# 8-wide heads: three bank pairs in a ring for scores and turned scores, four row strips of scores at once, and the turned maximum in the projections' bank

## The reference

```python
q = (query @ Wq.T + bq).reshape(b, s, 16, 8).transpose(0, 2, 1, 3)   # k and v likewise, from the context
scores = einsum('bhqd,bhkd->bhqk', q, k) / sqrt(8)
scores = where(mask, scores, very_low)       # layer 0: |query - key| <= 64; layer 2: a mask that is an input
out = einsum('bhqk,bhkd->bhqd', softmax(scores), v)
x = x + out.transpose(0, 2, 1, 3).reshape(b, s, 128) @ Wo.T + bo
```

## Time and profile before

| | us |
|---|---|
| median of 3 runs | 2033.67 |
| lowest and highest of them | 2032.84, 2035.79 |
| span of the profiled execution | 2027.5 |
| PE, DVE, ACT, POOL busy in it | 1766.7, 1092.1, 891.5, 652.9 |
| weight loads (PEld) busy | 1258.1 |

### The profile page before, as it was taken

One profiled execution on the slowest core, in us unless ns is written; L12 is line 12 of the kernel. 1 busy time (PEld: TensorE's weight loads), 2 busy tenths in 40 slices (PEclk: granted clock), 3 DMA queues, 4 the chain that ended last, 5 costly groups with the idle time before them and its releaser, 6 DMA issues.

```text
span 2027.5 us, 48497 instructions
## 1 busy us (share of the span) xinstructions
PE 1766.7 (87%) x18886; PEld 1258.1 (62%) x18886; DVE 1092.1 (54%) x3147; ACT 891.5 (44%) x2432; POOL 652.9 (32%) x656
## 2 busy tenths in 40 slices
PE   6999985587869999998999971999699999999978
PEld 3565564576648778873565551999456666666753
DVE  4666657567532222214566763656465656665548
ACT  2333320476334444432333320666265555556525
POOL 3233201467311111103214426455133233333405
PEclk8999996788679999997999995999799999999969
DMA  5000000000000000007210001222200000000001
GB/s 174 7 13 8 2 2 9 28 16 1 1 6 1 1 2 2 1 1 293 104 76 18 18 18 45 61 57 58 90 17 17 17 17 17 6 1 1 1 1 42
DMA packets 48828, 63.55 MB, mean 31 GB/s; under 512 B 8106, under 2 KB 37701, under 8 KB 48349
## 3 DMA queue, kind: packets, MB, share of 16 engines
q1 hardware_dynamic: 44253, 51.98, 7.8%
q0 software_dynamic: 4352, 8.47, 1.3%
HBM read 32.29 MB, written 28.65 MB: 30 GB/s over the span
## 4 chain that ended last, share of the span: by engine, by line
PE 57%; DVE 9%; issue 7%; POOL 4%; POOLq 3%; DVEq 2%; ACT 1%; DMA 1%; SPq 1%; PEldq 0%; PEld 0%; ACTq 0%
PE single L1835 5%; PE quad L1823 5%; PE pair L570 3%; PE single L621 3%; PE single L2156 3%; PE quad L2139 2%; PE quad L2145 2%; PE pair L1796 2%; PE quad L598 2%; PE pair L2519 2%; POOL tokens_by_expert L417 2%; DVE arena L768 1%; PE quad L2554 1%; PE quad L2545 1%; PE single L2531 1%
## 5 line engine op out<-in xcount | busy, mean ns | idle before, releaser
L768 DVE TENSOR_REDUCE arena<-pair 128x8 f32<-128x1024 f32 x128 | 156.7, 1224 | 140.4 <-PE pair L570 138.4
L2757 POOL TENSOR_TENSOR arena<-arena 128x512 f32<-128x512 f32 x128 | 130.4, 1040 | 296.2 <-DVE arena L2676 296.2
L263 POOL TENSOR_TENSOR rstd<-var_eps,neg_half 128x4 f32<-128x4 f32 (+1 forms) x64 | 65.5, 1024 | 350.3 <-DVE var_eps L259 266.7
L748 ACT ACTIVATE arena<-quad 128x1024 f32<-128x1024 f32 x128 | 124.1, 1021 | 69.3 <-PE quad L604 65.0
L1908 ACT ACTIVATE arena<-quad,arena 128x256 f32<-128x256 f32 x256 | 110.7, 475 | 98.1 <-PE quad L1823 98.1
L892 POOL TENSOR_SCALAR arena<-arena 128x512 f32<-128x512 f32 x56 | 86.7, 1565 | 196.6 <-ACT arena L690 196.5
L570 PE MATMUL pair<-arena 32*128 32x512 f32 x512 | 147.3, 652 | 0.0
L1999 DVE TENSOR_TENSOR arena<-single,arena 128x512 f32<-128x512 f32 x32 | 22.1, 692 | 206.2 <-PE single L1835 206.2
L2612 ACT ACTIVATE arena<-pair,arena 128x128 f32<-128x128 f32 x256 | 90.9, 381 | 89.0 <-DVE arena L2671 89.0
L2612 ACT ACTIVATE arena<-quad,arena 128x128 f32<-128x128 f32 x256 | 90.9, 381 | 86.4 <-DVE arena L2671 86.4
L1835 PE MATMUL single<-wide,arena 128*64 128x128 f32 x2048 | 123.9, 275 | 0.0
(11 more groups left out here) (502 smaller groups left out, 4376.7 us busy)
## 6 DMA issues: line engine op xcount, KB each, us to landing
tokens_by_expert<-arena SPq DMA_DIRECT2D x22, 780.0 KB, 8.6
arena<-in_ctxT SPq DMA_DIRECT2D x32, 256.0 KB, 3.0
arena<-tokens_by_expert SPq DMA_DIRECT2D x72, 65.0 KB, 1.8
wide<-in_w SPq DMA_DIRECT2D x2, 2048.0 KB, 10.1
arena<-outputs_by_choice SPq DMA_DIRECT2D x16, 256.0 KB, 4.1
wide<-in_wgu SPq DMA_DIRECT2D x1, 2736.0 KB
x<-in_x SPq DMA_DIRECT2D x4, 512.0 KB, 7.9
out_x<-x SPq DMA_DIRECT2D x8, 256.0 KB, 2.3
```

The source lines that it names most:

```text
L748: act.activation(probs[n % 2][:, 8 * p:8 * p + 8, :].rearrange("p h q -> p (h q)"), T[:, 1024 * p:1024 * p + 1024], ACT.Exp).then_inc(s["s ...
L768: dve.tensor_reduce(mx[m % 2][:, 8 * p:8 * p + 8], S[:].rearrange("p (h k) -> p h k", h=8), AX.X, ALU.max).then_inc(s["s_free"], 1)
L2757: pool.tensor_tensor(part, part, inv[t % 3][:, 4 * r:4 * r + 4].unsqueeze(2).broadcast_to([P, 4, P]), ALU.mult).then_inc(s["norm_ready"], 1)
```

## The change

The six banks of `S` and `T` become a ring of three pairs, `fours`. Sequence `m` has the pairs `m % 3` and `(m + 1) % 3`, for its scores and later for its turned scores. The scores of all four strips are issued in one go, after both mask pairs, and signalled once (`s_ready` counts sequences); DVE takes both maxima one behind the other. The turned scores of `n` wait for both exponentials of `n - 1` and, for their second pair of banks, for the first maximum of `n + 1`; the scores of `n + 2` wait for the second maximum of `n + 1` and the first exponential of `n`. The turned maximum goes through bank `M` like the projections, and `m_order` lists the users of `M` in their order: each waits until the one before has been read out. PE's order within an iteration is new, ACT's follows it, and on DVE the moments of a group come right behind its residual (`j` = 2) instead of one sequence later. The rest of `small_heads` and all other phases stay.

```diff
-            S, T, O, M = pair, quad, bank[6], bank[7]
+            fours = [pair[:, 0:1024], quad[:, 0:1024], quad[:, 1024:2048]]
+            T, O, M = quad, bank[6], bank[7]
             lg_part, count_part = O[:, 320:352], O[:, 384:512]
...
+            def halves(m):
+                return fours[m % 3], fours[(m + 1) % 3]
+            def bank_of(m, r):
+                return halves(m)[r // 2][:, 512 * (r % 2):512 * (r % 2) + 512]
+            def m_order():
+                yield "turn", 0
+                yield "turn", 1
+                yield "mt", 0
+                for n in range(N):
+                    g, j = divmod(n, G)
+                    if j == 3 and g + 2 < NG:
+                        yield "turn", g + 2
+                    if j == 0 and routes(g):
+                        yield "rows", g - 2
+                    if n + 1 < N:
+                        yield "mt", n + 1
+                    if j == 0 and g + 1 < NG:
+                        yield "q", g + 1
+                    if j == 1 and g >= 1:
+                        yield "out", g - 1
+                    if j == 2 and g + 1 < NG:
+                        yield "v", g + 1
+                    if j == 3 and g + 2 < NG:
+                        yield "k", g + 2
+                yield "out", NG - 1
+            m_emptied = {"turn": s["xnT_ready"], "mt": s["mts_ready"], "q": s["q_evac"], "v": s["v_evac"],
+                         "k": s["k_evac"], "out": s["x_done"]}
+            if l == 2:
+                m_emptied["rows"] = s["rt_copied"]
+            m_list = list(m_order())
+            m_before = dict(zip(m_list[1:], m_list))
+            def m_take(pe, key):
+                if key in m_before:
+                    kind, i = m_before[key]
+                    pe.wait_ge(m_emptied[kind], i + 1)
+                return M
...
                 def turn_rows(g):
                     pe.wait_ge(s["xr_ready"], g + 1)
-                    pe.wait_ge(s["k_evac"], min(g + 4, NG))
-                    pe.wait_ge(s["x_done"], g + 1)
-                    for j in range(G):
-                        mm = pe.transpose(M[:, j * P:(j + 1) * P], xr[:, g * G + j, 0:P], ident[:])
+                    dst = m_take(pe, ("rows", g))
+                    for j in range(G):
+                        mm = pe.transpose(dst[:, j * P:(j + 1) * P], xr[:, g * G + j, 0:P], ident[:])
...
                     pe.wait_ge(s["xn_ready"], g + 1)
-                    if g >= 2:
-                        pe.wait_ge(s["x_done"], g - 2)
-                    elif g == 1:
-                        pe.wait_ge(s["xnT_ready"], 1)
-                    for j in range(G):
-                        mm = pe.transpose(M[:, j * P:(j + 1) * P], xn[g % 2][:, j, :], ident[:])
+                    dst = m_take(pe, ("turn", g))
+                    for j in range(G):
+                        mm = pe.transpose(dst[:, j * P:(j + 1) * P], xn[g % 2][:, j, :], ident[:])
...
                     pe.wait_ge(s[f"ctx_in{g % 2}"], 16 * (g // 2 + 1))
-                    if g >= 2:
-                        pe.wait_ge(s["xnT_ready"], g + 1)
...
                     pe.wait_ge(s["xnT_ready"], g + 1)
-                    if g >= 2:
-                        pe.wait_ge(s["k_evac"], g + 1)
-                    if routes(g - 1):
-                        pe.wait_ge(s["rt_copied"], g - 2)
...
-                    pe.wait_ge(s["v_evac"], min(g + 3, NG))
                     pe.wait_ge(s["o_free"], G * g + G)
-                    if g == NG - 1:
-                        pe.wait_ge(s["x_done"], g)
-                    for j in range(G):
-                        mm = pe.matmul(M[:, j * P:(j + 1) * P], attnT[g % 2][:, j, :], wo[:], start=True, stop=True)
+                    dst = m_take(pe, ("out", g))
+                    for j in range(G):
+                        mm = pe.matmul(dst[:, j * P:(j + 1) * P], attnT[g % 2][:, j, :], wo[:], start=True, stop=True)
...
-                def mask_scores(m, p):
-
-                    pe.wait_ge(s["s_free"], 2 * m + p)
-                    mask_banks(pe, [S[:, r * 512:(r + 1) * 512] for r in range(2)], mask_bias[l]["S"])
-
-                def scores(m, p):
+                def scores(m):
                     g, j = divmod(m, G)
-                    if j == 0 and p == 0:
+                    if j == 0:
                         pe.wait_ge(s["q_evac"], g + 1)
                         pe.wait_ge(s["kv_ready"], g + 1)
-                    for r in range(2):
-                        rows = strip(2 * p + r)
-                        mm = pe.matmul(S[:, r * 512:(r + 1) * 512], qT[g % 2][rows, j * P:(j + 1) * P],
-                                       kv[g % 2][rows, j, :, :].rearrange("p a k -> p (a k)"),
+                    if m >= 1:
+                        pe.wait_ge(s["s_free"], 2 * m)
+                    mask_banks(pe, [bank_of(m, 0), bank_of(m, 1)], mask_bias[l]["S"])
+                    if m == 0:
+                        pe.wait_ge(s["k_evac"], 2)
+                    elif m == 1:
+                        pe.wait_ge(s["v_evac"], 1)
+                    else:
+                        pe.wait_ge(s["st_free"], 2 * (m - 2) + 1)
+                    mask_banks(pe, [bank_of(m, 2), bank_of(m, 3)], mask_bias[l]["S"])
+                    for r in range(4):
+                        mm = pe.matmul(bank_of(m, r), qT[g % 2][strip(r), j * P:(j + 1) * P],
+                                       kv[g % 2][strip(r), j, :, :].rearrange("p a k -> p (a k)"),
                                        start=False, stop=True, skip_group_check=True)
                     mm.then_inc(s["s_ready"], 1)
                 def turn_max(m):
                     pe.wait_ge(s["mhl_ready"], m + 1)
-                    if m >= 1:
-                        pe.wait_ge(s["mts_ready"], m)
-                    if m >= 3:
-                        pe.wait_ge(s["o_free"], m - 2)
-                    pe.transpose(O[:, 256:320].bitcast(BF16), mhl[m % 2], identb[:]).then_inc(s["mt_ready"], 1)
-
-                def mask_turned(n):
+                    dst = m_take(pe, ("mt", m))
+                    pe.transpose(dst[:, 0:64].bitcast(BF16), mhl[m % 2], identb[:]).then_inc(s["mt_ready"], 1)
+                def turned(n):
+                    g, j = divmod(n, G)
                     if n == 0:
-                        pe.wait_ge(s["k_evac"], 2)
-                        pe.wait_ge(s["q_evac"], 1)
-                        pe.wait_ge(s["v_evac"], 1)
-                    pe.wait_ge(s["st_free"], 2 * n)
-                    for r in (0, 2):
-                        mask_banks(pe, [T[:, i * 512:(i + 1) * 512] for i in (r, r + 1)], mask_bias[l]["T"])
-
-                def turned(n):
-
-                    g, j = divmod(n, G)
+                        pe.wait_ge(s["s_free"], 1)
+                    else:
+                        pe.wait_ge(s["st_free"], 2 * n)
+                    mask_banks(pe, [bank_of(n, 0), bank_of(n, 1)], mask_bias[l]["T"])
+                    pe.wait_ge(s["s_free"], min(2 * n + 3, 2 * N))
+                    mask_banks(pe, [bank_of(n, 2), bank_of(n, 3)], mask_bias[l]["T"])
                     for a in range(4):
                         for r in range(4):
-                            pe.matmul(T[:, r * 512 + a * P:r * 512 + (a + 1) * P], kv[g % 2][strip(r), j, a, :],
+                            pe.matmul(bank_of(n, r)[:, a * P:(a + 1) * P], kv[g % 2][strip(r), j, a, :],
                                       qT[g % 2][strip(r), j * P:(j + 1) * P], start=False, stop=False,
                                       skip_group_check=True)
                     pe.wait_ge(s["mts_ready"], n + 1)
                     for a in range(4):
                         for r in range(4):
-                            mm = pe.matmul(T[:, r * 512 + a * P:r * 512 + (a + 1) * P], chooser[strip(r), a, :],
+                            mm = pe.matmul(bank_of(n, r)[:, a * P:(a + 1) * P], chooser[strip(r), a, :],
                                            mts[n % 2][strip(r), :], start=False, stop=True, skip_group_check=True)
...
-                    pe.wait_ge(s["mts_ready"], min(m + 3, N))
...
                 for m in range(2):
-                    for p in range(2):
-                        mask_scores(m, p)
-                        scores(m, p)
+                    scores(m)
                 pe.wait_ge(s["cvec_ready"], 1)
                 turn_max(0)
                 for n in range(N):
                     g, j = divmod(n, G)
+                    turned(n)
+                    if j == 3 and g + 2 < NG:
+                        turn(g + 2)
                     if j == 0 and routes(g):
                         turn_rows(g - 2)
-                    if j == 0 and g + 1 < NG and l == 0:
-                        project_q(g + 1, M)
-                    elif j == 1 and g + 1 < NG:
-                        project_v(g + 1, M)
-                    elif j == 2 and g >= 1:
-                        output(g - 1)
```

(61 more changed lines are left out.)

4 lines of the change are left out of this document (1 added, 3 removed).

## The result

| us | before | after |
|---|---|---|
| median of the runs | 2033.26 (4 runs) | 1955.46 (4 runs) |
| lowest, highest | 2032.60, 2035.79 | 1953.65, 1958.94 |
| span of the profiled execution | 2027.5 | 1953.0 |
| PE, DVE, ACT busy in it | 1766.7, 1092.1, 891.5 | 1697.6, 1086.3, 890.3 |

The ratio is 0.9625 [0.9609, 0.9641], 77.8 us less where 70 were forecast, and inside the range of 1951 to 1992. The profiled execution after took 1954.56, 1.5 above its span.

A forecast was written before the change was run, and what follows sets the result against it. TensorE was taken to set the pace in the attention of layers 0 and 2. Layer 0's loop 30, layer 2's 25 and the starts 15 made 70 us off, giving 1963.7 us, range 1951 to 1992.

The forecast's parts named there:

- Four strips cost what two cost: Attention scores: one set of four strips takes 1.06 us instead of two pairs, 1.01 us less per sequence.
- The second rival: Four strips do not overlap: scores cost 2.1 us, about 16 us off in all, 2018 us; chance 0.06.
- The interval: Layer 0, per sequence: 6.63 us including 0.08 of added wait, 7.2 with a transposition, against 7.59 ordinary before.
- PE's sum of 6.55: TensorE's own work per ordinary sequence: turned scores 1.22, attention 1.88, turned maximum 0.16, masks twice 0.57, scores 1.06, projection 1.09.
- The moments: Moved next to the residual, they make normalising late once per group: 2.5 us given back in layer 0, 1.5 in layer 2.
- The turned maximum in `M`: Sharing one bank with the projections costs nothing; without cover up to 0.3 us a sequence plus the copy.
- Layer 2: Sequences 1 to 31: 28 us less after late normalisings, 25 after clock falls; routing groups 32.8 us each.
- The two or three falls of the clock: Layer 2: more idling in the routing groups drops the clock to 1.2 GHz, costing 3 us in all.
- The starts: Start of attention in layers 0 and 2: 7.5 us less each, 5 at worst, 9 at best, 15 for both.
- What lies behind: Stages after the attentions: the scatters move with their barrier and hide nothing, so no gain or loss.
- The waits take half: Rival: disturbances or clock falls lengthen each interval by 0.45 us, loops gain 27 instead of 55, 1991 us; chance 0.17.
- Slower, by the clock: Rival: waits drop the clock to 1.2 GHz in the loop; with 20 sequences hit, 2076 us; chance 0.04.

The follow-up runs named there:

- the repeat of before: The kernel before, unchanged, executed once more for a second profile: 2013.34 us, span 2011.8.
- the experiment with both edits: Kernel after with the turned maximum in bank `O` behind the projection and the moments back at `j` = 3: 1938.76 us, 0.9612 of the kernel before.

## Why the prediction was right, and where it was off

*Four strips cost what two cost.* Forecast 1.06, measured 1.07. The second rival falls by this row alone; the experiment with two strips at a time, which has its masks in another order, shows about what it would have cost: 89 us.

*The interval.* Forecast 6.63 and 7.2, measured 6.76 and 7.34. That the wait for the first maximum sets it was right: from scores to turned scores 2.80 were forecast and 2.83 came (70.95 to 73.78). In 53 of the 58 intervals that begin with sequences 1 to 29 of the two layers the second mask pair starts 2.49 us behind the scores. The step that was off is PE's sum of 6.55: turned scores were carried over at 1.22 from a place where the next matmuls, a score pair, had the same tiling. Now attention follows, with another, and they take 1.32. Where the change reorders PE, the price of a tiling change moves with the order. The added wait was counted at 0.08; the second masks take 0.67 where the first take 0.56, so it is 0.11, and the experiment that waits for both maxima shows that the cover is what holds it there. Over layer 0's 23 ordinary and six long intervals this makes 3.8 us. The working also read some 0.4 us of waiting into the 0.83 before the turned maximum; by its own prices, 0.45 + 0.22 for masks and 0.12 for the change of tiling, only 0.04 is left. Nothing in its sum rests on that.

*The moments.* Booked at 2.5 in layer 0 and 1.5 in layer 2, for normalising that comes late. That step failed: layer 0's intervals at `j` = 2 are 6.76 like the others, and moving the moments back changes nothing there and costs 0.7 to 1.0 in a routing group. The two errors in layer 0 nearly cancel, which is luck: 203.5 measured, 202.3 forecast.

*The turned maximum in `M`* was costed at nothing, and ACT's part is indeed hidden. At its new place bank `O` would cost 1.6 us a sequence.

*Layer 2.* Forecast for its groups 20.5, 27.1, 28.7, 32.8, 28.7, 32.8, 28.5, 20.5; measured 20.86, 27.62, 29.09, 32.20, 29.19, 32.27, 28.52, 20.35. The two or three falls of the clock, booked at 3, did not come: none lies in either loop, in any of the three profiles of this kernel. That and the moments are the 4 us by which 28.9 exceeds 25. The Trainium skill's rule in TensorEngine Tiling (Array Packing), PSUM Bottleneck, does not bind in layer 0, where DVE has 4.9 us of work in 6.76 (it is the delay of one maximum that PE meets there, not DVE's load); in the routing groups, with DVE busy 24.7 of 32.2 and PE 2.2 short of full, the trace goes with it.

*The starts.* This is the term that was mis-sized: 13.0 and 11.3 for 7.5 each, above even the bound of 9. The timeline of the kernel after, TensorE, start of layer 0, as the earlier trace rows:

```profile
16.95 1.12 PE L573 MATMUL quad<-arena,wq 128*128 128x512 f32 x2 [0.69 <-ACT arena L718]
...
19.33 0.40 PE L156 MATMUL pair<-maskS0own,identb 64*64 64x512 bf16 x1
...
23.58 0.40 PE L156 MATMUL quad<-maskS0own,identb 64*64 64x512 bf16 x1 [2.55 <-DVE arena L787]
...
26.62 0.40 PE L156 MATMUL quad<-maskS0own,identb 64*64 64x512 bf16 x1 [0.81 <-DVE arena L787]
...
26.96 0.38 PE L630 MATMUL pair<-arena 32*128 32x128 f32 x2
```

Two things are in it. From the first masks to the turned scores of sequence 0 it is 7.63 where the working had 9.4: it took PE's second set at low clock, 2.1, and this profile has full clock there, 1.14. And the masks begin at 19.33 instead of 21.61, ahead of the first instruction that the change touches: the same projection took 2.07 in the profile of before and 1.12 here, and in the repeat of before 1.13, with masks at 19.50. That part is the execution's and not the change's. From masks to sequence 1 the start is 25.0 in both profiles of before and 14.3 in all three of the kernel after, 10.7 less; in layer 2 it is 25.1 and 25.0 against 15.6, 15.0 and 15.1, about 10. But the clock has a share in that. The busy table of this start, of the kernel before, of the kernel after, and of the experiment with both edits, whose code up to there does the same work (the granted clock is third from the end):

```profile
21.61:46.61 25.00, 19.62 (x162) 7.48 (x165) 10.95 (x26) 5.14 (x9) 6.25 (x5) 0.73 0.57 216
```

```profile
19.33:33.64 14.31, 10.34 (x150) 4.61 (x152) 10.54 (x21) 4.16 (x7) 8.05 (x6) 1.00 0.81 298
```

```profile
19.64:38.65 19.01, 15.35 (x149) 6.30 (x152) 11.25 (x25) 4.15 (x7) 8.04 (x6) 0.64 0.74 275
```

Before and in that experiment the clock is at 1.2 GHz for some 13.7 us of it. With the clock alike, then, the new start is 6.0 us shorter, inside the forecast's 5 to 9, and 4.7 of the 10.7 are that the clock stayed up. It was down for 13.7 us in all four starts of the two profiles of before, and for so long in one of the eighteen starts of the nine profiles that issue four strips at once, so the change seems to bring this too; why is not shown.

*What lies behind.* Nothing was booked; +3.2 and +4.7 came. The first is in every profile of the new code. The busy table, expert stage behind layer 0, of the kernel before, then of the kernel after:

```profile
286.24:341.57 55.33, 41.68 (x169) 32.40 (x170) 38.74 (x165) 5.58 (x10) 7.05 (x7) 0.73 0.00 1
```

```profile
244.34:302.82 58.48, 45.98 (x169) 36.81 (x170) 38.73 (x165) 5.59 (x10) 7.05 (x7) 0.65 0.00 1
```

The same 169 matmuls run in the same order at a mean clock of 0.65 instead of 0.73. Both profiles of before have 3.4 us at 2.4 GHz some 8 us behind the barrier; the ten profiles of the changed kernel and its variants go down to 1.2 GHz within 5 us of the barrier and stay there for 27.3 us without a break, and all take 58.5. That holds whether the loop ahead was slow or quick. What in the new code keeps the clock down there was not found, and no run was made for it. The stage behind layer 2 varies between 704 and 721 us with unchanged code, in both kernels.

*The sum.* 74.5 us on the span for 70: the starts and loops brought 12.1 more than forecast, and what lies behind took 7.9 of that back, 4.7 of them not the change's. That the total came so close is in part luck. The other 3.3 of the 77.8 come from the offset between span and median, 6.2 before, where it was left standing, and 2.5 after. The time lies near the end of the range for which the working names starts at full clock and no falls, and that is what happened.

*The rivals.* "The waits take half" needed 0.45 us more per interval; there was 0.13, and PE waited for POOL in none of the intervals read. "Slower, by the clock" did not occur, and the experiment with the maximum in `O`, which ends 2.3% above the kernel before, is slower by its waits first (103 us of the 120) and by the clock second.

## What to carry to other kernels

Small matmuls on 32 rows each are worth issuing four strips at a time, even at 512 columns, as soon as there are banks for them, and a ring of pairs finds these banks if the reader of one pair is finished before the writer needs both. Wait for the half that is needed, not for the whole: here that one constant is 1.1 us a sequence, as much as the strips. Look for the path that sets the interval, here from turned scores over attention to scores, and from there over the first maximum: the small turned maximum cost its full 0.16 us on it and nothing in the shadow of the wait, while time saved in that shadow brings nothing. And keep an instruction out of a bank whose reader stands just ahead of it.

## What the runs showed of the hardware that was not expected

- Four fp32 strips of 512 columns into four banks start within 20 ns of each other and take 1.07 us, as two do (1.06).
- The turned scores take 0.1 us more where a matmul of another tiling follows (1.22 to 1.32); projection and turned maximum, which have the same, take 0.11 less side by side than apart.
- The clock did not fall with a wait of 0.1 us in 6.76, nor in the routing groups with PE idle for 2.2 of 32.2 us. With the maximum in `O` it fell once in layer 0, with a fifth of idle in waits of up to 1.9 us, and twelve times in layer 2, with a fifth of idle and waits of up to 3.4. The Trainium skill, TensorE: Matmul & The Clock Gate, in its section on psum-queue depth-cycling, ties such swings to short pauses between groups over alternating banks. The ring alternates banks in every sequence and holds 2.4 GHz, so the alternation alone does not bring the swings; which pauses do is not settled here.
- A busy PE is no safeguard either. With two strips at a time, the clock fell once in layer 2 right behind a stretch in which the profile has PE busy without a break (busy table, in which the ends of matmuls are modelled; the granted clock is third from the end):

```profile
1087.40:1090.80 3.40, 3.40 (x25) 1.64 (x25) 1.35 (x3) 0.28 (x1) 3.21 (x3) 1.00 0.00 0
1090.80:1094.20 3.40, 3.40 (x12) 0.69 (x10) 2.63 (x4) 0.69 (x1) 1.44 (x2) 0.50 0.12 39
```

- The start of layer 0's attention, with the same work for each engine, was profiled at full clock (five profiles), and with stretches at 1.2 GHz of 3.4 us (two) and 13.7 us (one); with that, sequence 1 began at 33.5 to 38.7 us. A difference of 5 us between two single executions of such kernels may be no more than this.
